# A weight staging copy after every fourteenth attention step instead of every ninth

## The chip, the cores and the metric

The kernel runs on the 8 cores of one Trainium2 chip. Each core takes 1,024 of the 8,192 tokens and runs the same program; nothing is exchanged between cores. The metric is the device time of the slowest core in microseconds (us).

## The reference

A layer in three parts, on x of 2 x 4096 tokens and 4096 features:

```python
x = x + 0.5 * ffn(layernorm(x))     # low-rank experts, rank 8*16 = 128, softmax router over 8
x = x + attn(layernorm(x))          # 32 heads of 128, 8 KV heads, 8192 cached keys
x = x + 0.5 * ffn(layernorm(x))

def attn(h):
    q = rope(h @ Wq)                          # Wq 4096 x 4096
    K, V = kv_cache[block_table]              # 8 KV heads, each serves 4 query heads
    ctx = softmax(q @ K.T / sqrt(128)) @ V
    return ctx @ Wo                           # Wo 4096 x 4096
```

## The kernel before

Activations lie transposed: 32 tiles of 128 features by 512 tokens. A core's 1,024 tokens are two chunks of 512, and the chunks run one after the other (`for c in range(NCH)`). A chunk is: layer norm (`emit_LN`), low-rank part (`emit_FFN`), layer norm, query projection with rotation (`emit_QT`), attention (`emit_ATT`), output projection (`emit_WO`, called WO below), layer norm, low-rank part, store. Instructions are put by hand on one in-order stream for each engine (`PE`, `AC`, `DV`, `GP` for GpSimd, which the profile calls POOL, and `SY` for SyncE, which it calls SP); waits are counts of semaphores.

**Attention.** There are 8 KV heads g, for each 4 query heads, and for each of these 32 groups of two key blocks. A group is two score matmuls (L511), one exponential over both (L518), two matmuls that sum the weights (L539) and two that apply the values (L551), these four in `flush_group`, which runs two groups late. So a chunk has 8 x 4 x 32 = 1,024 calls of `flush_group`, 128 for each g, and `flushctr` counts them. Keys and values of one g fill `KT` and `VT`, in 4 slabs of 16 blocks. There is no second buffer: a slab of g + 1 is loaded by GP (L472, L479) once the fourth query head of g is through with the slab of g, that is at calls 103, 111, 119 and 127 of the 128. For the last g nothing is loaded, so the last slab of a chunk is issued at call 895.

**Staging copies.** Both projections need a weight matrix in bf16. In chunk 0 the query projection reads it from the f32 input, with a cast in the DMA. For the rest (WO of both chunks, the query projection of chunk 1) the kernel makes bf16 copies in DRAM during chunk 0. The queue `pc_queue` holds 64 blocks of wo and then 64 of wq. `precast_pump(1)` takes one block: GP issues a casting load of 512 KB as counted after the cast, wo or wq to the one buffer `PCB` (L458), which waits until PCB is free; SP issues the plain store from PCB to `wob` or `wqb` (L464), which waits for the load; PCB is free when the store has landed. So the copies are one serial chain, load, store, load, and each load sits in GP's stream in front of whatever GP is to do next. None of them waits for the progress of attention. GP's stream is put together in program order, so a pump stands between the slab loads as the call counter places it.

What is left in `pc_queue` after the last call of `flush_group` is issued at once (`while pc_queue: precast_pump(1)`), in GP's stream ahead of the squares of the next layer norm. WO reads `wob` with DMAs of ACT's queue into the two halves of `WB`, and waits for the copies of wo alone (`pco_done.get("o")`). WO adds each result tile to X on DVE (L626).

**Layer norm.** For each of 32 tiles: DVE casts X to XN (L198), GP squares it into the single buffer `SQr` (L202), PE sums both (L209, L217). The square of a tile waits until PE has read the one before.

Of the kernel before, what the change touches and what calls it, by code (L numbers as in the profile page):

```python
# [73 lines left out]
def build_program():  # L74
# [35 lines left out]
    with ctx:  # L110
# [46 lines left out]
        def bw(b):  # L157
            return free.get(("pb", b))

        def tile(buf, i, w=CH):  # L160
            return buf[:, i * w:(i + 1) * w]
# [286 lines left out]
        def precast_pump(n=1):  # L448
            for _ in range(n):
                if not pc_queue:  # L450
                    return
                which, blk = pc_queue.pop(0)
                i, hh = blk // 2, blk % 2
                w_d = wo_d if which == "o" else wq_d
                dst_d = wob_d if which == "o" else wqb_d
                osem = sPCOo if which == "o" else sPCOq
                GP.add(
                    (lambda i=i, hh=hh, w_d=w_d: lambda g: g.dma_start(  # L458
                        PCB[:, :].rearrange("p (j m) -> p j m", j=16),
                        w_d.rearrange("(j p) m -> p j m", p=128)  # L460
                        [:, hh * 16:(hh + 1) * 16, i * 128:(i + 1) * 128]))(),
                    waits=[free.get(("pcb",))], inc=sPCI, inc_amt=16)
                v = SY.add(
                    (lambda blk=blk, dst_d=dst_d: lambda s: s.dma_start(  # L464
                        dst_d[blk], PCB[:, :]))(),
                    waits=[(sPCI, sPCI.val)], inc=osem, inc_amt=16)
                free[("pcb",)] = (osem, v)
                pco_done[which] = (osem, v)

        def emit_kv_slab(c, g, s, ktv, vtv):  # L470
            v = GP.add(
                (lambda g=g, s=s: lambda gp: gp.dma_start(  # L472
                    KT[:, s * SLAB * 128:(s + 1) * SLAB * 128],
                    kt_d[g * 128:(g + 1) * 128,
                         s * SLAB * 128:(s + 1) * SLAB * 128]))(),
                waits=[free.get(("kvslab", s))], inc=sKT[s], inc_amt=16)
            ktv[(g, s)] = (sKT[s], v)
            v = GP.add(
                (lambda g=g, s=s: lambda gp: gp.dma_start(  # L479
                    VT[:, s * SLAB * 128:(s + 1) * SLAB * 128]  # L480
                    .rearrange("p (j d) -> p j d", j=SLAB),
                    vt_d.rearrange("(j p) d -> p j d", p=128)
                    [:, g * NK + s * SLAB:g * NK + (s + 1) * SLAB, :]))(),
                waits=[free.get(("kvslab", s))], inc=sVT[s], inc_amt=16)
            vtv[(g, s)] = (sVT[s], v)
# [5 lines left out]
        flushctr = [0]  # L491

        def emit_ATT(c, po_qt):
# [32 lines left out]
            def flush_group(item):  # L526
                g, qh, grp, gg, ac_e = item
                h = g * 4 + qh
                cb = 2 + (h % 2)
                lb = 4 + (h % 2)  # L530
                slot = (2 * gg) % NPS
                pe_L = pe_ctx = None
                for t in range(2):
                    j = 2 * grp + t
                    wl = [(sAC, ac_e)]
                    if j == 0:
                        wl.append(bw(lb))
                    pe_L = PE.add(
                        (lambda lb=lb, slot=slot, t=t, j=j: lambda tt: tt.matmul(  # L539
                            BNK[lb], ONES[:, :],  # L540
                            PS4[:, (slot + t) * CH:(slot + t + 1) * CH],
                            start=(j == 0), stop=(j == NK - 1)))(),
                        waits=wl, inc=(sPE if j == NK - 1 else None))
                    wc = [vtv[(g, j // SLAB)]]
                    if j == 0:
                        wc.append(bw(cb))
                    need_inc = (t == 1) and (
                        (qh == 3 and (j % SLAB) == SLAB - 1)
                        or grp == NK // 2 - 1)
                    pe_ctx = PE.add(  # L550
                        (lambda g=g, j=j, slot=slot, t=t, cb=cb: lambda tt: tt.matmul(  # L551
                            BNK[cb], VT[:, j * 128:(j + 1) * 128],
                            PS4[:, (slot + t) * CH:(slot + t + 1) * CH],
                            start=(j == 0), stop=(j == NK - 1)))(),
                        waits=wc, inc=(sPE if need_inc else None))
                    if qh == 3 and t == 1 and (j % SLAB) == SLAB - 1:
                        free[("kvslab", j // SLAB)] = (sPE, pe_ctx)
                        if g + 1 < NG:
                            emit_kv_slab(c, g + 1, j // SLAB, ktv, vtv)
                if flushctr[0] % 9 == 0:  # L560
                    precast_pump(1)
                flushctr[0] += 1
                if grp == NK // 2 - 1:
                    ac_lnl = AC.add(
                        (lambda lb=lb: lambda sc: sc.activation(
                            MB[:, :], BNK[lb], AF.Ln))(),
                        waits=[(sPE, pe_L), free.get(("mb",))], inc=sAC)
                    free[("pb", lb)] = (sAC, ac_lnl)
                    ac_rl = AC.add(lambda sc: sc.activation(  # L569
                        RSD[:, :], MB[:, :], AF.Exp, scale=-1.0),  # L570
                        waits=[(sAC, ac_lnl), free.get(("rsd",))], inc=sAC)
                    free[("mb",)] = (sAC, ac_rl)
                    dv_c = DV.add(
                        (lambda h=h, cb=cb: lambda v: v.tensor_tensor(  # L574
                            tile(QC, h), BNK[cb], RSD[:, :], ALU.mult))(),
                        waits=[(sPE, pe_ctx), (sAC, ac_rl)], inc=sDV)
                    free[("pb", cb)] = (sDV, dv_c)
                    free[("rsd",)] = (sDV, dv_c)
                    dv_ctx[h] = dv_c

            for g in range(NG):
                for qh in range(4):
                    for grp in range(NK // 2):
                        gg, ac_e = emit_scores_group(g, qh, grp)
                        pending.append((g, qh, grp, gg, ac_e))
                        if len(pending) > 2:
                            flush_group(pending.pop(0))
                while pending:
                    flush_group(pending.pop(0))
# [186 lines left out]
```

How the kernel before makes its waits and increments, by code:

```python
    def replay(self, eng):  # L63
        for fn, waits, inc, amt in self.ops:
            for s, v in waits:
                eng.wait_ge(s.h, v)
            if fn is None:
                continue
            instr = fn(eng)
            if inc is not None:
                instr.then_inc(inc.h, amt)
```

## Time and profile before

| | us |
|---|---|
| median of 3 runs | 4906.14 (4897.51 to 5272.22) |
| profiled execution, device time | 4920.42 |
| its slowest core, span (core 0) | 4918.9 |
| spans of the 8 cores | 4845.2 to 4918.9 |
| mean granted clock of TensorE, 8 cores | 0.901 to 0.908 |

The engines over that span: PE busy 4061.0 us (83%), ACT 2345.8 us (48%), POOL 776.0 us (16%), DVE 686.7 us (14%). The rows below come from core 0 of this execution unless their caption names another. A "wait" row says how long an engine was idle ahead of an instruction until the named releaser; a timeline row gives start, duration, instruction, and in brackets the idle time ahead of it. A DMA instruction on POOL is its issue; its bytes land later.

### The profile page before, as it was taken

What the parts mean: (1) busy time and instruction counts of PE and PEld (TensorE: products, weight loads), DVE (VectorE), ACT (ScalarE), POOL (GpSimd) and SP (SyncE); (2) the same over time, 40 slices, a digit from 0 to 9 for tenths busy, and PEclk for the clock granted to TensorE, in tenths of its full rate; (3) what the DMA queues carried; (4) which work ended last, traced back from release to release, by engine and by line L of the source; (5) the groups of instructions that cost most, each with busy time, mean ns of one, the idle gap of its engine ahead of it and who ended that gap; (6) DMA issues with size and microseconds to landing.
All of it is one profiled execution on the core that took longest, in us unless ns stands there. A gap on an engine that the chain in (4) does not pass through costs nothing.

```text
span 4918.9 us, 46299 instructions; the slowest of 8 cores (4845.2 to 4918.9 us)
## 1 busy us (share of the span) xinstructions
PE 4061.0 (83%) x16880; PEld 1701.4 (35%) x17224; DVE 686.7 (14%) x937; ACT 2345.8 (48%) x2193; POOL 776.0 (16%) x722
## 2 busy tenths in 40 slices
PE   2556669999999899896773549999999999999985
PEld 0112224444444344342320114444444444444431
DVE  2531120000000000000026553300000000000025
ACT  0000008787788787770000000088888888887000
POOL 4541120111111111100023560000000000000004
PEclk9768789999999999998975559999999999999995
DMA  4148886766776776767614015302220221120432
GB/s 82 17 44 77 77 86 103 105 95 101 112 111 97 111 100 99 106 106 162 159 64 150 13 32 153 120 1 35 35 26 9 35 35 15 20 35 20 140 115 77
DMA packets 616055, 378.54 MB, mean 77 GB/s; under 512 B 549024, under 2 KB 549024, under 8 KB 615840
## 3 DMA queue, kind: packets, MB, share of 16 engines
q0 software_dynamic: 551392, 174.22, 34.3%
q10 hardware_dynamic: 27360, 99.63, 6.0%
q1 hardware_dynamic: 37088, 101.73, 5.4%
q8 instruction: 147, 2.41, 0.2%
q14 instruction: 68, 0.56, 0.0%
HBM read 465.83 MB, written 83.89 MB: 112 GB/s over the span
## 4 chain that ended last, share of the span: by engine, by line
PE 46%; DMA 35%; POOL 9%; issue 5%; ACT 2%; DVE 1%; SPq 1%; another core or an unknown queue 0%; POOLq 0%; ACTq 0%; DVEq 0%
DMA PCB<-wo 12%; PE pc L551 9%; PE pl L539 9%; PE psA L615 7%; PE psA L422 7%; DMA PCB<-wq 6%; PE psA L511 5%; PE psB L511 5%; DMA wob<-PCB 5%; DMA WB<-wq 4%; POOL SQr L202 4%; DMA WB<-wob 4%; DMA wqb<-PCB 3%; POOL XN L260 2%; PE pl L217 2%
## 5 line engine op out<-in xcount | busy, mean ns | idle before, releaser
L518 ACT ACTIVATE PS<-psA,CST 128x1024 bf16<-128x1024 f32 x1024 | 1139.8, 1113 | 1014.2 <-PE psA L511 1007.0
L551 PE MATMUL pc<-PS,VT 128*128 128x512 bf16 x4013 | 1531.2, 382 | 7.9 <-DMA VT<-vt 3.6
L539 PE MATMUL pl<-PS,ONES 128*128 128x512 bf16 x4013 | 1532.8, 382 | 4.6 <-issue 0.2
L518 ACT ACTIVATE PS<-psB,CST 128x1024 bf16<-128x1024 f32 x1024 | 1140.6, 1114 | 198.9 <-PE psB L511 188.6
L422 PE MATMUL psA<-XN,WB 128*128 128x512 bf16 x2008 | 535.8, 426 | 222.3 <-DMA WB<-wq 148.3
L511 PE MATMUL psA<-QC,KT 128*128 128x512 bf16 x2006 | 607.2, 383 | 105.4 <-DMA KT<-kt 73.6
L511 PE MATMUL psB<-QC,KT 128*128 128x512 bf16 x2010 | 608.5, 383 | 7.4 <-DVE UR L376 5.2
L551 PEld LDWEIGHTS pc<-PS,VT 128*128 128x128 bf16 x4096 | 403.1, 98 | 497.5 <-issue 21.2
L539 PEld LDWEIGHTS pl<-PS,ONES 128*128 128x128 bf16 x4096 | 403.4, 98 | 491.9 <-issue 16.4
L615 PE MATMUL psA<-QC,WB 128*128 128x512 bf16 x2006 | 475.4, 394 | 91.6 <-DMA WB<-wob 85.6
L238 ACT ACTIVATE G<-RSD,CST 128x512 f32<-128x512 f32 x6 | 4.3, 721 | 1017.0 <-DVE RSD L232 1017.0
L574 DVE TENSOR_TENSOR QC<-pc,RSD 128x512 bf16<-128x512 f32 x64 | 44.3, 692 | 2763.0 <-ACT RSD L569 2763.0
L422 PEld LDWEIGHTS psA<-XN,WB 128*128 128x128 bf16 x2048 | 213.6, 106 | 541.2 <-issue 364.4
L202 POOL TENSOR_TENSOR SQr<-XN 128x512 bf16<-128x512 bf16 x192 | 210.8, 1098 | 789.0 <-DVE XN L198 626.6
L615 PEld LDWEIGHTS psA<-QC,WB 128*128 128x128 bf16 x2048 | 200.2, 100 | 367.0 <-issue 161.5
L511 PEld LDWEIGHTS psA<-QC,KT 128*128 128x128 bf16 x2048 | 195.5, 98 | 364.1 <-issue 142.6
L511 PEld LDWEIGHTS psB<-QC,KT 128*128 128x128 bf16 x2048 | 202.1, 99 | 252.7 <-issue 15.6
L217 PE MATMUL pl<-SQr,ONES 128*128 128x512 bf16 x188 | 109.4, 582 | 181.9 <-POOL SQr L202 181.9
L472 POOL DMA_DIRECT2D KT<-kt x64 | 36.1, 564 | 1371.8 <-PE pc L551 1371.8
L209 PE MATMUL pl<-XN,ONES 128*128 128x512 bf16 x190 | 119.0, 626 | 90.3 <-DVE XN L198 85.2
L458 POOL DMA_DIRECT2D PCB<-wq x64 | 73.2, 1144 | 751.0 <-DMA wqb<-PCB 713.6
L458 POOL DMA_DIRECT2D PCB<-wo x64 | 73.3, 1146 | 737.4 <-DMA wob<-PCB 719.1
(57 smaller groups left out, 1401.6 us busy)
## 6 DMA issues: line engine op xcount, KB each, us to landing
WB<-wob ACTq DMA_DIRECT2D x128, 512.0 KB, 3.3
WB<-wq POOLq DMA_DIRECT2D x66, 512.0 KB, 7.3
KT<-kt POOLq DMA_DIRECT2D x64, 512.0 KB, 10.4
VT<-vt POOLq DMA_DIRECT2D x64, 512.0 KB, 14.1
PCB<-wo POOLq DMA_DIRECT2D x64, 512.0 KB, 7.8
wob<-PCB SPq DMA_DIRECT2D x64, 512.0 KB, 3.0
PCB<-wq POOLq DMA_DIRECT2D x64, 512.0 KB, 8.3
wqb<-PCB SPq DMA_DIRECT2D x64, 512.0 KB, 3.4
```

The lines of the kernel that those rows point to most:

```text
L202: (lambda i=i: lambda g: g.tensor_tensor(SQr[:, :], tile(XN, i), tile(XN, i), ALU.mult))(),
L209: (lambda i=i: lambda t: t.matmul(BNK[4], ONES[:, :], tile(XN, i), start=(i == 0), stop=(i == DT - 1)))(),
L217: (lambda i=i: lambda t: t.matmul(BNK[5], ONES[:, :], SQr[:, :], start=(i == 0), stop=(i == DT - 1)))(),
L260: (lambda i=i, sl=sl: lambda e: e.tensor_tensor(tile(XN, i), tile(TTr, sl), RSDB[:, :], ALU.mult))(),
L422: (lambda i=i, j=j, b=b: lambda t: t.matmul(BNK[b], WB[:, (0 if j < 16 else 2048) + (j % 16) * 128: (0 if j < 16 else 2048) + (j % 16) * 1 ...
L458: (lambda i=i, hh=hh, w_d=w_d: lambda g: g.dma_start(PCB[:, :].rearrange("p (j m) -> p j m", j=16), w_d.rearrange("(j p) m -> p j m", p=12 ...
L511: (lambda j=j, b=lo + t, h=h: lambda tt: tt.matmul(BNK[b], KT[:, j * 128:(j + 1) * 128], tile(QC, h), start=True, stop=True))(),
L518: (lambda slot=slot, big=big: lambda sc: sc.activation(PS4[:, slot * CH:(slot + 2) * CH], big[:, :], AF.Exp, bias=CST[:, 0:1], scale=ISQ))(),
L539: (lambda lb=lb, slot=slot, t=t, j=j: lambda tt: tt.matmul(BNK[lb], ONES[:, :], PS4[:, (slot + t) * CH:(slot + t + 1) * CH], start=(j == 0 ...
L551: (lambda g=g, j=j, slot=slot, t=t, cb=cb: lambda tt: tt.matmul(BNK[cb], VT[:, j * 128:(j + 1) * 128], PS4[:, (slot + t) * CH:(slot + t + ...
L574: (lambda h=h, cb=cb: lambda v: v.tensor_tensor(tile(QC, h), BNK[cb], RSD[:, :], ALU.mult))(),
L615: (lambda i=i, j=j, b=b: lambda t: t.matmul(BNK[b], WB[:, (0 if j < 16 else 2048) + (j % 16) * 128: (0 if j < 16 else 2048) + (j % 16) * 1 ...
```

## The change

The pump is called after every fourteenth call of `flush_group` instead of every ninth:

```diff
@@ -557,7 +557,7 @@
                         free[("kvslab", j // SLAB)] = (sPE, pe_ctx)
                         if g + 1 < NG:
                             emit_kv_slab(c, g + 1, j // SLAB, ktv, vtv)
-                if flushctr[0] % 9 == 0:
+                if flushctr[0] % 14 == 0:
                     precast_pump(1)
                 flushctr[0] += 1
                 if grp == NK // 2 - 1:
```

The number of copies (128) and their order stay. Counted from the code, for the calls 0 to 1,023 of chunk 0:

| | every 9th | every 14th |
|---|---|---|
| pumps placed in attention | 114 | 74 |
| pumps per g (128 calls) | 14.2 | 9.1 |
| pumps ahead of the last slab load (call 895) | 100 | 64 |
| pumps behind the last slab load | 28 | 64 |
| of these behind the last call | 14 | 54 |

## Rows read from the trace of the kernel before

**Rows 1.** Page, the chain that ended last: shares by line.

```profile
DMA PCB<-wo 12%; PE pc L551 9%; PE pl L539 9%; PE psA L615 7%; PE psA L422 7%; DMA PCB<-wq 6%; PE psA L511 5%; PE psB L511 5%; DMA wob<-PCB 5%; DMA WB<-wq 4%; POOL SQr L202 4%; DMA WB<-wob 4%; DMA wqb<-PCB 3%; POOL XN L260 2%; PE pl L217 2%
```

**Rows 2.** Waits of POOL, whole span: us in total, times, longest.

```profile
POOL KT L472 <- PE pc L551: 1371.8, 28, 377.5
POOL PCB L458 <- DMA wob<-PCB: 728.8, 63, 36.6
POOL PCB L458 <- DMA wqb<-PCB: 713.6, 61, 16.0
```

**Rows 3.** Stages, both attentions, WO of both chunks: us, busy, PEclk, DMA share, GB/s.

```profile
733.00:2195.00 1462.00, 1358.89 (x6022) 604.42 (x6144) 25.60 (x38) 1166.39 (x1088) 174.83 (x167) 0.97 0.71 103
2197.00:2510.00 313.00, 241.84 (x972) 99.77 (x992) 21.23 (x31) 0.00 (x0) 18.29 (x16) 0.91 0.67 159
3181.00:4530.00 1349.00, 1324.45 (x6014) 598.68 (x6138) 24.22 (x36) 1166.04 (x1086) 47.81 (x56) 1.00 0.18 23
4535.00:4780.00 245.00, 228.73 (x1008) 97.86 (x1029) 27.44 (x42) 0.00 (x0) 3.16 (x3) 0.99 0.40 135
```

**Rows 4.** Waits of PE from 720 to 2200 us, the attention of chunk 0.

```profile
PE psA L511 <- DMA KT<-kt: 73.6, 17, 6.7
```

**Rows 5.** Timeline of POOL, copies away from slab loads and beside one.

```profile
957.13 1.14 POOL L458 DMA_DIRECT2D PCB<-wo  x1 [9.56 <-DMA wob<-PCB]
...
1047.84 1.14 POOL L458 DMA_DIRECT2D PCB<-wo  x1 [9.79 <-DMA wob<-PCB]
...
2038.12 1.15 POOL L458 DMA_DIRECT2D PCB<-wq  x1 [12.79 <-DMA wqb<-PCB]
2039.25 0.56 POOL L472 DMA_DIRECT2D KT<-kt  x1
2039.80 1.17 POOL L479 DMA_DIRECT2D VT<-vt  x1
2056.12 1.15 POOL L458 DMA_DIRECT2D PCB<-wq  x1 [15.16 <-DMA wqb<-PCB]
```

**Rows 6.** DMA issues from 957 to 1048 us: count, KB each, us to landing.

```profile
PCB<-wo POOLq DMA_DIRECT2D x9, 512.0 KB, 7.5
wob<-PCB SPq DMA_DIRECT2D x8, 512.0 KB, 3.1
```

**Rows 7.** Timeline of POOL: end of attention, WO of chunk 0, next layer norm.

```profile
2184.52 1.15 POOL L458 DMA_DIRECT2D PCB<-wq  x1 [11.19 <-DMA wqb<-PCB]
...
2403.79 1.15 POOL L458 DMA_DIRECT2D PCB<-wq  x1 [12.96 <-DMA wqb<-PCB]
2518.50 1.08 POOL L202 TENSOR_TENSOR SQr<-XN 128x512 bf16<-128x512 bf16 x1 [113.56 <-DVE XN L198]
```

**Rows 8.** Timeline of POOL, slab loads of keys: slab 0, slab 0, chunk 1's last.

```profile
874.98 0.56 POOL L472 DMA_DIRECT2D KT<-kt  x1
...
1063.14 0.56 POOL L472 DMA_DIRECT2D KT<-kt  x1
...
4363.42 0.55 POOL L472 DMA_DIRECT2D KT<-kt  x1 [7.79 <-PE pc L551]
```

**Rows 9.** Page, issues of keys and values: count, KB each, us to landing.

```profile
KT<-kt POOLq DMA_DIRECT2D x64, 512.0 KB, 10.4
VT<-vt POOLq DMA_DIRECT2D x64, 512.0 KB, 14.1
```

**Rows 10.** Score matmuls of each attention: count, duration ns, first and last start.

```profile
L511 PE MATMUL psA<-QC,KT x1003: 376/379/634, 733.0 to 2188.3; 128*128 128x512 bf16 x168
...
L511 PE MATMUL psA<-QC,KT x162: 376/379/634, 3180.3 to 3398.6; 128*128 128x512 bf16 x162
```

**Rows 11.** Timeline of DVE: WO columns 0, 15, 31 of chunk 0.

```profile
2206.24 0.69 DVE L626 TENSOR_TENSOR X<-psA,X 128x512 f32<-128x512 f32 x1 [11.55 <-PE psA L615]
...
2393.77 0.69 DVE L626 TENSOR_TENSOR X<-psA,X 128x512 f32<-128x512 f32 x1 [9.32 <-PE psA L615]
...
2517.33 0.69 DVE L626 TENSOR_TENSOR X<-psA,X 128x512 f32<-128x512 f32 x1 [7.11 <-remote]
```

**Rows 12.** Timeline of POOL: squares of that layer norm, first with the casts beside, then without.

```profile
2520.37 1.07 POOL L202 TENSOR_TENSOR SQr<-XN 128x512 bf16<-128x512 bf16 x1 [0.78 <-PE pl L217]
...
2535.08 1.30 POOL L202 TENSOR_TENSOR SQr<-XN 128x512 bf16<-128x512 bf16 x1 [0.88 <-PE pl L217]
2537.26 1.04 POOL L202 TENSOR_TENSOR SQr<-XN 128x512 bf16<-128x512 bf16 x1 [0.88 <-PE pl L217]
2539.18 1.04 POOL L202 TENSOR_TENSOR SQr<-XN 128x512 bf16<-128x512 bf16 x1 [0.88 <-PE pl L217]
```

**Rows 13.** Copies of wq on cores 0 and 7: duration ns, first and last issue.

```profile
L458 POOL DMA_DIRECT2D PCB<-wq x64: 1140/1142/1157, 1569.9 to 2403.8; - x64
...
L458 POOL DMA_DIRECT2D PCB<-wq x64: 1140/1140/1154, 1527.8 to 2325.4; - x64
```

## The prediction

> **What bounds the kernel now.** I read the chain that ended last first. Four of its entries are staging copies, PCB<-wo, PCB<-wq, wob<-PCB and wqb<-PCB, 26% of the span together [rows 1]. TensorE is busy 83% of the time, yet the chain goes through loads and stores that no matmul of that stage reads. The waits of POOL say why: ahead of 124 of the 128 copy loads it idled for 1,442 us in all, each time until the store of the copy before had landed [rows 2]. So in chunk 0 GP is a serial chain of copies, and everything else in its stream, the slab loads among it, is as late as that chain.
>
> The stages come next. The two attentions do the same work and take 1,462 and 1,349 us [rows 3]; from the first score matmul to the last that is 2188.3 - 733.0 = 1,455 us in chunk 0. In chunk 1 there are no copies, the clock is 1.00 and PE is busy 98% of the stage: that is the attention as PE alone would have it. In chunk 0 PE idled 73.6 us for keys [rows 4], and the clock is 0.97. The two WO stages take 313 and 245 us [rows 3], the first with copies beside it.
>
> The timeline gives the rate of the copies. Away from slab loads, 8 intervals from 957.13 to 1047.84 are 11.3 us each [rows 5]: 7.5 us until the load lands, 3.1 us for the store, and the issues [rows 6]. With a slab's two loads behind the copy it is 2056.12 - 2038.12 = 18.0 us [rows 5]. Beside WO, 16 intervals from 2184.52 to 2403.79 are 13.7 us each [rows 7].
>
> A check that these explain attention 0: 14.2 pumps for each g are 10.2 at 11.3 us and 4 at 18.0 us, 187 us. Slab 0 of g = 1 and of g = 2 were issued at 874.98 and 1063.14, 188 us apart [rows 8]. PE alone needs 1,349 / 8 = 168.6 us per g [rows 3]. So attention 0 runs at GP's pace, about 18 us per g over PE's.
>
> **The change part by part.** No instruction is added or removed; 40 pumps move from between the attention calls to behind them. As GP waits for nothing in a pump but PCB, only a slab load holds it back to PE's pace; after the last slab load (call 895) GP runs through all that is left. So what counts is the time of the last slab load, and the pumps behind it: 28 before, 64 after.
>
> *Step 1, attention.* With 9.1 pumps per g, GP needs at most 9.1 x 18.0 = 164 us and about 5.1 x 11.3 + 4 x 18.0 = 130 us, under PE's 168.6. GP then waits for PE at the slabs, as it does in chunk 1 [rows 2]. Is a slab still in time? It is released two groups late and is needed about 23 groups later, at 168.6 / 128 = 1.32 us a group some 30 us. Keys land in 10.4 us, values in 14.1 us [rows 9], and at most one copy, up to 18 us but in most cases already running, can stand before it. I take the wait for keys as about zero. The bound on the other side is that nothing is gained.
>
> In chunk 1 the last slab was issued 4363.42 - 3180.3 = 1,183 us after the first score matmul [rows 8, 10]. The new last slab is then at 733.0 + 1,183 = 1,916 us instead of 2,039.25 [rows 5], and attention ends at about 733 + 1,349 = 2,082 instead of 2,190. That is a gain of 108 us for the start of WO, and of 123 us for the start of the tail of copies.
>
> *Step 2, the tail.* The first of the 64 pumps is issued at 1,918; 63 intervals follow.
> - Until WO, at 2,086: one of 17 us with the slab beside it and 13 of 11.6 us (128.4 us for 11 intervals from 2056.12 to 2184.52, the same place before [rows 5, 7]), 168 us for 14.
> - Beside WO. Before, columns 0 to 15 of WO, all with copies beside them, took (2393.77 - 2206.24) / 15 = 12.5 us each [rows 11]. Now all 32 have copies beside them: 400 us, from 2,091 to 2,491. At 13.7 us that holds 29 intervals, to about 2,485.
> - The last 20 are alone. The nearest row is the quiet stretch, 11.3 us: 226 us.
> The last copy load is issued at 2,711 us, and the first square of the layer norm stands right behind it, at 2,712.
>
> *Step 3, what waits for it.* Before, GP had issued its last copy at 2403.79 and sat idle 113.56 us until WO's last tile was cast; the first square was at 2518.50 [rows 7]. The copies were free, with 114 us of cover. Now WO is done at 2,491 and the square waits 221 us more: PE's sums wait for the squares, the means for the sums, and the low-rank part, the store, the reload of X and all of chunk 1 for these. Nothing later has slack to take it up; every stage of chunk 1 is behind this one. The shift is 2,712 - 2518.5 = 193 us. The 32 casts on DVE are then long done. Before, the squares beside them came every 2.2 us and later ones every 1.92 us [rows 12]; 8 squares by 0.26 us give back 2 us. Sum: +191 us.
>
> *The gain of step 1 is inside this sum*, not beside it: it moves WO, which is hidden behind the tail, and it starts the tail earlier. The slowdown of WO, from 320 to 400 us, costs nothing, because the tail covers it with 221 us to spare; without that cover it would cost 80.
>
> The profiled execution took 4920.42 us, so its like would be 5,111. It stood 14 us over the median of 4906.14, so the forecast for the median is 5,097 us.
>
> *Bounds of the interval.* The tail is 63 intervals, and each 1 us on the mean is 63 us. All at 11.3 ends at 2,630 (+110 with the 2 us off); all at 13.7 ends at 2,781 (+261). My mean is (2,711 - 1,918) / 63 = 12.6 us. Cores differ: from the first to the last of the wq copies core 0 took 833.9 us and core 7 took 797.6 [rows 13], so 4% less; core 0 should again be the slowest. The Trainium skill (DMA: Bandwidth & Descriptors, section "Issuing engines are not separate DMA queues") says that transfers of all issuers share 16 engines and interleave. The rows agree: the copies slow from 11.3 to 13.7 us beside WO, and WO's columns stretch as well, though they are issued from ACT and the copies from POOL and SP.
>
> **The rivals.**
>
> *The tail is hidden* (the other side). If the copies are done by the time WO ends, nothing waits for them and only the earlier WO is left: 2,491 + 1 against 2518.5, so -26 us, 4,880, not slower. It decides at (2,491 - 1,918) / 63 = 9.1 us an interval. The shortest interval in the rows, idle time and issue together, is 9.56 + 1.14 = 10.7 us [rows 5], and beside WO it must be slower. What speaks for it is only that the cores' memory traffic is spread differently. 3%. The Trainium skill (same page, section "Anatomy of one DMA — SWDGE (gpsimd) path") puts a DMA at 2.0 us plus its bytes over 436e9 per second. For 512 KB that is an estimated 3.2 us, 6.4 us for load and store, and the tail would take 63 x 6.4 = 403 us and be hidden. The trace agrees for the store (3.1 us) and not for the casting load (7.5 us) [rows 6], so I hold to the rows.
>
> *The copies alone are quick.* Once WO is over, no other transfer of this core runs, and neither do the other cores' slab loads. If the last 20 take 10 us and those beside WO 12.5 (32 fit there), the tail ends at 2,491 + 17 x 10 = 2,661: +141 us, 5,047. 12%.
>
> *Attention gains nothing.* If keys come late for another reason, e.g. bandwidth, the last slab stays at 2,039 and the tail of 64 ends at 2,039 + 63 x 12.6 = 2,833: +314 us, 5,220. Against it speaks that attention 1 has no wait for keys with the same loads, and that the copies between slabs become fewer. Half of it (+60 on my number) is likelier than all. 5%.
>
> *The copies slow down.* WO with copies beside it throughout may hold the copies to 15 us or more: 27 fit beside WO, 22 follow, +23 us, 5,120; inside my range.
>
> **How the numbers follow.** The forecast's own mechanism, with intervals near the rows, has 80% and gives 5,060 to 5,140; the quick tail 12%, no gain in attention 5%, the hidden tail 3%. The range 5,045 to 5,150 takes in the quick tail and the slowed copies. This kernel's measurement can tell about 2% from no change, so slower means over 5,004: that takes a shift of 98 us, a mean interval over 11.1 us. The quiet rate is already 11.3 and a third of the tail is beside WO, so slower 94%, within 2% 5%, faster 1%.
>
> **What would show it.** In the profile after: (1) attention 0 takes about 1,350 us, PE's wait for keys there is near zero, and POOL waits at L472 for PE in chunk 0. (2) The last L472 of chunk 0 is near 1,916 us and 64 copy loads follow. (3) WO of chunk 0 ends near 2,490, with about 12.5 us a column to its end. (4) The first square of the next layer norm is at 2,712, right behind the last copy load, and POOL's idle time ahead of it is about zero instead of 114 us; PE idles there some 220 us. (5) From there on every stage takes as long as before. I am wrong if the last copy is issued before WO ends, or if the last slab is much later than 1,916.

## The result: slower by 4%, and the profile after

| | before | after |
|---|---|---|
| undisturbed runs, us | 4897.5 to 4920.3 | 5102.7 to 5124.3 |
| ratio of the undisturbed runs | | 1.0415, 95% interval 1.0392 to 1.0439 |
| span of the slowest core in the profiled execution, us | 4918.9 (core 0) | 5119.0 (core 0) |
| last slab load of chunk 0 (GP), us | 2039.25 | 1922.92 |
| last copy load (GP), us | 2403.79 | 2714.55 |
| last column of WO, chunk 0 (DVE), us | 2517.33 | 2481.53 |
| first square of the next layer norm, us | 2518.50 | 2715.71 |

The forecast was 5,097 us, 1.039 of the median before. (In some executions of either kernel the cores of a die had a lower clock and the time was hundreds of us longer; they are left out of every ratio here, and with them the median over the 10 runs after is 5213.36 us.) The other seven cores show the same shift: their first squares stand at 2,658 to 2,690 us, before at 2,438 to 2,496.

The waits of POOL after, whole span (us in total, times, longest), answer to [rows 2]:

```profile
POOL KT L472 <- PE pc L551: 1857.6, 53, 378.6
POOL PCB L458 <- DMA wqb<-PCB: 716.5, 63, 16.2
POOL PCB L458 <- DMA wob<-PCB: 528.3, 51, 31.0
```

GP now waits for PE ahead of 53 slab loads instead of 28: in chunk 0, too, it arrives early. The waits of PE from 720 to 2100 us no longer have keys among them; their longest row is the ordinary one for the exponential:

```profile
PE psA L511 <- ACT PS L518: 15.7, 30, 1.6
```

The stages after (us, busy time and count of PE, PE's weight loads, DVE, ACT and POOL, granted clock, DMA share, GB/s): attention of chunk 0, WO, the tail alone, and the start of the layer norm, answering to [rows 3]:

```profile
733.00:2090.00 1357.00, 1330.64 (x6036) 601.03 (x6160) 26.00 (x38) 1163.44 (x1086) 136.87 (x134) 1.00 0.61 85
2090.00:2500.00 410.00, 270.40 (x1008) 108.31 (x1027) 33.55 (x65) 1.23 (x2) 34.63 (x29) 0.85 0.76 157
2500.00:2700.00 200.00, 0.00 (x0) 0.00 (x0) 0.00 (x0) 0.00 (x0) 20.54 (x18) 0.50 0.63 94
2700.00:2820.00 120.00, 46.73 (x92) 9.04 (x93) 38.30 (x36) 1.35 (x2) 72.16 (x66) 0.50 0.13 22
```

The third row is the loss. For 200 us PE, DVE and ACT do nothing at all, and GP is busy 20.5 us issuing copies. The granted clock is at its lower level there (0.50, which is 1.2 GHz; PE stands still), and the mean over the span falls from 0.901 to 0.887. The lower mean is no second cause of the loss: from the first square to the end this core takes 2,403.3 us, before 2,400.4. The timeline of POOL at its end, with the last slab load and the first copy behind it at the head, answering to [rows 7]:

```profile
1922.92 0.55 POOL L472 DMA_DIRECT2D KT<-kt  x1 [7.79 <-PE pc L551]
...
1924.61 1.17 POOL L458 DMA_DIRECT2D PCB<-wq  x1
...
2083.89 1.14 POOL L458 DMA_DIRECT2D PCB<-wq  x1 [10.28 <-DMA wqb<-PCB]
...
2479.95 1.14 POOL L458 DMA_DIRECT2D PCB<-wq  x1 [11.17 <-DMA wqb<-PCB]
...
2714.55 1.15 POOL L458 DMA_DIRECT2D PCB<-wq  x1 [9.92 <-DMA wqb<-PCB]
2715.71 1.05 POOL L202 TENSOR_TENSOR SQr<-XN 128x512 bf16<-128x512 bf16 x1
2717.75 1.04 POOL L202 TENSOR_TENSOR SQr<-XN 128x512 bf16<-128x512 bf16 x1 [0.98 <-PE pl L217]
2719.66 1.04 POOL L202 TENSOR_TENSOR SQr<-XN 128x512 bf16<-128x512 bf16 x1 [0.88 <-PE pl L217]
```

The first square has no bracket: GP did not idle ahead of it at all, where before it had 113.56 us to spare [rows 7]. Its input had long been there. The timeline of DVE shows WO's first and last columns and the casts behind them, done at 2,493 us:

```profile
2106.33 0.69 DVE L626 TENSOR_TENSOR X<-psA,X 128x512 f32<-128x512 f32 x1 [13.37 <-PE psA L615]
...
2481.53 0.69 DVE L626 TENSOR_TENSOR X<-psA,X 128x512 f32<-128x512 f32 x1 [9.03 <-remote]
2482.13 10.81 DVE L198 CAST XN<-X 128x512 bf16<-128x512 f32 x32
```

From there the shift is handed on unchanged. Chunk 1's first score matmul was at 3180.3 us [rows 10]; after it is the first of this row (count, duration in ns, first and last start):

```profile
L511 PE MATMUL psA<-QC,KT x1003: 376/379/631, 3378.6 to 4725.0; 128*128 128x512 bf16 x168
```

That is 198 us later, against 197 us for the first square and 200 us for the span.

### The profile page after: what moved, and what is told of

Same layout as the page of the kernel before. It is cut to its first block, busy times and chain, and to the rows that moved or that the text cites. A ratio compares the mean times of both kernels' runs of the same rounds, so it can differ in the third digit from the quotient of the medians.

```text
span 5119.0 us, 46299 instructions; the slowest of 8 cores (5063.1 to 5119.0 us)
## 1 busy us (share of the span) xinstructions
PE 4044.6 (79%) x16880; PEld 1699.6 (33%) x17224; DVE 679.8 (13%) x937; ACT 2342.9 (46%) x2193; POOL 774.4 (15%) x722
## 4 chain that ended last, share of the span: by engine, by line
PE 60%; DMA 22%; POOL 8%; issue 5%; ACT 2%; DVE 1%; SPq 1%; POOLq 0%; ACTq 0%; another core or an unknown queue 0%; DVEq 0%
PE pc L551 15%; PE pl L539 15%; DMA PCB<-wq 10%; PE psA L511 8%; PE psB L511 8%; PE psA L422 7%; DMA WB<-wq 5%; DMA wqb<-PCB 4%; POOL SQr L202 4%; PE psA L615 4%; POOL XN L260 2%; PE pl L217 2%; POOL TTr L256 2%; ACT PS L518 2%; DMA WB<-wqb 1%
## 5 line engine op out<-in xcount | busy, mean ns | idle before, releaser
L615 PE MATMUL psA<-QC,WB 128*128 128x512 bf16 x2006 | 497.6, 406 | 137.3 <-DMA WB<-wob 131.2
L217 PEld LDWEIGHTS pl<-SQr,ONES 128*128 128x128 bf16 x192 | 20.0, 104 | 561.2 <-issue 561.2
```

Of the source, the lines that this page charges most:

```text
L217: (lambda i=i: lambda t: t.matmul(BNK[5], ONES[:, :], SQr[:, :], start=(i == 0), stop=(i == DT - 1)))(),
L615: (lambda i=i, j=j, b=b: lambda t: t.matmul(BNK[b], WB[:, (0 if j < 16 else 2048) + (j % 16) * 128: (0 if j < 16 else 2048) + (j % 16) * 1 ...
```

## The experiments

Each kernel ran beside the kernel before on one chip, in the same rounds; ratios are to the kernel before. The theory (A): GP's in-order stream is the schedule. In attention the slowest of GP's chain and PE sets the pace; behind the last slab load GP runs the rest of the copies without a break, and the layer norm starts when both that tail and WO are over. The rivals: the slowed WO is what costs (B in the first run), copies cost wherever they are made outside attention (B in the second and third), the count of fourteen hurts as such.

### The copies left over are not made

Behind attention, and in chunk 1's query projection:

```diff
-            while pc_queue:
-                precast_pump(1)
+            pc_queue.clear()
@@
-                                wqb_d[2 * i + hh]))(),
+                                wqb_d[(2 * i + hh) % 10]))(),
```

> Every fourteenth call, and the 54 copies left over behind attention are not made at all; chunk 1's query projection reads the ten copied blocks of wq over and over, so its reads are as many and as large but its output is wrong. Theory A (the tail stands in GP's stream ahead of the squares, and that alone costs the time): WO starts near 2,090 us, takes some 245 to 260 us once the 10 copies placed in the last g are done, the first square is near 2,345 instead of 2,716 us, and the time is about 370 us under the changed kernel, 4,735 to 4,760, ratio to before 0.965 to 0.97. Theory B (the loss is in WO, slowed from 313 to about 400 us by copies beside it): only some 150 us come back, 4,950 or more.

Measured: ratio 0.9647 (0.9533 to 0.9761), span 4747.0 us, 372 us under the changed kernel, where 370 was expected. The timeline of POOL on the slowest core:

```profile
2024.13 1.14 POOL L458 DMA_DIRECT2D PCB<-wq  x1 [9.86 <-DMA wqb<-PCB]
2334.00 1.08 POOL L202 TENSOR_TENSOR SQr<-XN 128x512 bf16<-128x512 bf16 x1 [308.73 <-DVE XN L198]
```

The square is where WO lets it be. B falls: had only WO's stretch been the loss, some 150 us would have come back. But this run takes away position and traffic of the copies at once; the third run parts them.

### Eleven instead of fourteen

```diff
-                if flushctr[0] % 9 == 0:
+                if flushctr[0] % 11 == 0:
```

> A pump after every eleventh call: 82 ahead of the last slab load and 46 behind it. Theory A: GP still waits for PE at the slabs (about 158 us of copies and slabs for each g against 168.6), the last slab is near 1,925 us, 45 intervals of about 12.7 us end near 2,497, just when WO with copies beside it ends (2,490). The first square is at 2,495 to 2,510 and the time 10 to 25 us under before, ratio 0.995 to 0.998. Theory B (time grows with each copy moved from attention into or behind WO): 18 of the 36 moved copies cost half of the loss, about 100 us over before, ratio 1.02.

Measured: ratio 1.003 (1.0009 to 1.0052), span 4942.3 us. A missed by some 30 us (it wanted a time under that of before), and B by more (it wanted 1.02). The timelines of DVE and of POOL say where A missed:

```profile
2450.81 0.69 DVE L626 TENSOR_TENSOR X<-psA,X 128x512 f32<-128x512 f32 x1 [6.60 <-PE psA L615]
...
2527.46 1.15 POOL L458 DMA_DIRECT2D PCB<-wq  x1 [8.62 <-DMA wqb<-PCB]
2528.62 1.05 POOL L202 TENSOR_TENSOR SQr<-XN 128x512 bf16<-128x512 bf16 x1
```

The last slab was at 1,909 us, the first copy behind it at 1,930, and the 45 intervals took 13.3 us each on the mean, not 12.7; the tail ended 30 us after the time expected. WO ended at 2,451 rather than 2,490. So the tail, though expected to be even with WO, outlived it by 77 us. The mechanism stands, and a difference of two long terms was sized too finely.

### The same copies, the last 23 of them inside the layer norms

Fourteen again. 31 copies are issued behind attention; `emit_LN` takes the rest, in the three layer norms ahead of chunk 1's query projection:

```diff
-            while pc_queue:
-                precast_pump(1)
+            if c == 0:
+                precast_pump(31)
@@ emit_LN, behind the square and its matmul; behind a normalisation on GP
+                if spread and i % 6 == 5:
+                    precast_pump(1)
+                    if spread and i in (8, 16, 24):
+                        precast_pump(1)
```

> Every fourteenth call, with only 31 of the leftover copies issued behind attention; the other 23 are placed in GP's stream inside the next three layer norms, one after every sixth square and three among the normalisations, about 11 us apart. The copies and their traffic are those of the changed kernel, all before the query projection of chunk 1. Theory A: the squares start when WO ends, near 2,490 us, 23 issues of 1.15 us in GP's stream cost 27 us and some short waits for the buffer 10 to 30 more; time 4,900 to 4,950, ratio 1.00 to 1.01, against 1.04 of the changed kernel. Theory B (the copies cost time wherever they lie outside attention): it stays at 1.03 to 1.045.

Measured: ratio 0.9977 (0.995 to 1.0003). All 128 copies are made, 64 of them behind the last slab load as in the changed kernel, and its loss is gone. The timeline of POOL on the slowest core:

```profile
2473.81 1.08 POOL L202 TENSOR_TENSOR SQr<-XN 128x512 bf16<-128x512 bf16 x1 [46.34 <-DVE XN L198]
...
2483.83 1.31 POOL L202 TENSOR_TENSOR SQr<-XN 128x512 bf16<-128x512 bf16 x1 [0.88 <-PE pl L217]
2485.09 1.44 POOL L462 DMA_DIRECT2D PCB<-wq  x1
2486.54 1.09 POOL L202 TENSOR_TENSOR SQr<-XN 128x512 bf16<-128x512 bf16 x1
```

A copy between two squares delays them by less than its issue takes: 2483.83 to 2486.54 is 2.7 us, where 2.2 us lie between two squares without it. It waits for nothing, since some 12 us lie between two copies and its buffer is free again. Over the three layer norms the 23 copies cost 13 to 20 us (from the first square to chunk 1's query projection this core takes 400 us, the cores of the kernel before 380 to 387). So it is not the copies' traffic, nor that they are made outside attention. It is that in the changed kernel they stand in GP's stream in one block ahead of work that needs GP.

### A second buffer for the copies

```diff
+                k = pc_n[0] % 2
+                pc_n[0] += 1
+                buf = PCB[:, :] if k == 0 else XN[:, 0:2048]
+                isem, osem = sPCI[k], sPCO[(which, k)]
@@
-                if flushctr[0] % 9 == 0:
+                if flushctr[0] % 8 == 0:
```

Load and store use `buf`, `isem` and `osem`. Whoever waited for the copies of a matrix waits for both semaphores, and the casts of the next layer norm into these four tiles wait for the last store out of them.

> A second buffer for the copies (the first four tiles of XN, which nothing uses from the query projection to the next layer norm), with semaphores of its own, so that a load runs while the copy before is stored; a pump after every eighth call, so all 128 are placed in attention. Theory A (a chain of load and store, 7.5 + 3.1 us, sets the rate): a copy takes about 8 us, 16 copies and 4 slabs of a g fit under PE's 168.6 us, attention 0 takes 1,350 us, no copy is left beside WO, which takes 245 us; 108 + 68 us less than before, about 4,735, ratio 0.965. Theory C (the DMA engines set the rate, busy 71% of attention 0 before): a copy stays at 10 us or more, keys come late, attention 0 stays over 1,420 us and the time over 4,830.

Measured: ratio 0.9659 (0.9585 to 0.9733), span 4749.3 us, the fastest kernel of the study that computes the whole result. The stages on its slowest core, attention of chunk 0 and WO, columns as above:

```profile
733.00:2090.00 1357.00, 1328.78 (x6028) 600.17 (x6152) 24.34 (x36) 1165.18 (x1088) 191.90 (x182) 1.00 0.87 123
2090.00:2335.00 245.00, 224.18 (x997) 96.73 (x1016) 23.89 (x35) 0.00 (x0) 1.08 (x1) 1.00 0.40 133
```

All 128 copies now fit beside an attention at PE's pace. The DMA engines are busy 87% of it, against 71% before [rows 3], and keys are still in time. C falls. The 15 intervals behind the last slab load have a mean of 7.5 us. This run changes the buffer and the count at once; the run with fourteen and the second buffer, below, keeps the changed kernel's count.

### Ten and eight instead of nine

The same line as in the second run, with 10 and with 8.

> A pump after every tenth call: 12.8 for each g, 90 ahead of the last slab load and 38 behind it. Theory A (both sides of the balance decide, GP's pace in attention and the tail behind it): 8.8 copies at 11.2 us and 4 with slabs at 17.5 us are 169 us for each g, just PE's 168.6, so attention 0 takes 1,350 to 1,365 us; the tail of 37 intervals at 13 us ends near 2,410, before WO does (near 2,455); first square near 2,460 us, time 45 to 60 us under before, ratio 0.988 to 0.991, better than nine, eleven or fourteen. Theory B (more copies in attention are always the better): at or over before, ratio 1.00.

> A pump after every eighth call: 16 for each g, 112 ahead of the last slab load and 16 behind it. Theory A: 12 copies at 11.3 us and 4 at 18 us are 208 us for each g, 40 over PE's; the last slab comes near 2,150 us, attention ends near 2,320 us, the 16 copies left are done near then, and WO has the DMA engines nearly to itself, 250 us; first square near 2,575 us, 55 us over before, ratio 1.01 to 1.015. Theory B (thinner pumps are what hurts in the changed kernel, denser ones help): under before, ratio below 1.

Measured: ten 0.993 (0.9896 to 0.9965), eight 1.0135 (1.0083 to 1.0188). With ten the attention is at PE's pace and the tail ends 54 us before the square can start (timeline of POOL, slowest core):

```profile
2420.18 1.15 POOL L458 DMA_DIRECT2D PCB<-wq  x1 [11.66 <-DMA wqb<-PCB]
2475.30 1.08 POOL L202 TENSOR_TENSOR SQr<-XN 128x512 bf16<-128x512 bf16 x1 [53.98 <-DVE XN L198]
```

The ratio is a little short of the 0.988 to 0.991 expected, since WO ended at 2,474 and not at 2,455. With eight the tail is short, and the loss is in attention instead, in the waits of PE from 720 to 2330 us:

```profile
PE psA L511 <- DMA KT<-kt: 180.4, 27, 14.1
```

So the time is lowest in between and rises to both sides: 1.0135, 1, 0.993, 1.003, 1.0415 for 8, 9, 10, 11 and 14. No theory in which more copies beside attention are always better, or always worse, gives this.

### Fourteen with the second buffer

> The changed kernel's count of fourteen with the second buffer and its semaphores: the same 64 copies behind the last slab load, but a load runs while the copy before is stored. Theory A (what hurts is the length of the tail, so it is harmless where a copy is quick): beside attention 7.5 us a copy as with the second buffer before, beside WO 9 to 10 us; 22 copies until WO starts, the other 42 end near 2,480 us, WO ends between 2,430 and 2,490; first square within 10 us of WO's end, time 30 to 80 us under before, ratio 0.985 to 0.995. Theory B (the count of fourteen hurts by itself): over before, ratio 1.02 or more.

Measured: ratio 1.0011 (0.9988 to 1.0034), span 4909.8 us. The count is that of the changed kernel, 64 copies stand behind the last slab load, and the loss is gone: the tail takes 8.3 us a copy instead of 12.5 and ends at 2,435, ahead of WO (timelines of POOL and of DVE, slowest core):

```profile
2435.14 1.15 POOL L465 DMA_DIRECT2D XN<-wq  x1 [2.16 <-DMA wqb<-XN]
2484.73 1.08 POOL L204 TENSOR_TENSOR SQr<-XN 128x512 bf16<-128x512 bf16 x1 [48.45 <-DVE XN L199]
...
2483.56 0.69 DVE L636 TENSOR_TENSOR X<-psA,X 128x512 f32<-128x512 f32 x1 [7.20 <-remote]
```

The count does not hurt by itself, only through the length of the tail. The time missed the expected 0.985 to 0.995: WO's columns took (2483.56 - 2102.59) / 31 = 12.3 us with the copies beside them, so WO ended at the late end of the range given. Attention ended about 100 us earlier than in the kernel before and the first square came 34 us earlier: some two thirds of that gain had gone into a slower WO. Of the 34 us only 9 are left in the span, since this core takes 2,425 us from its first square to the end, and the cores of the kernel before 2,400 to 2,416. That difference stays unexplained.

### The same bytes in long runs

```diff
-                        PCB[:, :].rearrange("p (j m) -> p j m", j=16),
-                        w_d.rearrange("(j p) m -> p j m", p=128)
-                        [:, hh * 16:(hh + 1) * 16, i * 128:(i + 1) * 128]))(),
+                        PCB[:, :],
+                        w_d[i * 128:(i + 1) * 128,
+                            hh * 2048:(hh + 1) * 2048]))(),
```

> The changed kernel, but each copy load reads 128 rows of 2,048 neighbouring f32 instead of 16 runs of 128 f32 in each partition, with the same bytes and the same cast; the copies hold other blocks of the matrices, so the output is wrong. Theory A (short runs make the casting load take 7.5 us): the load lands in 3 to 5 us, a copy takes 7 to 8.5 us alone, the tail of 64 ends near 2,430 us, before WO does, and the time is at or under before, ratio 0.985 to 1.0. Theory D (the cast or the memory makes it 7.5 us): the load stays at 7 us or more and the ratio stays near 1.04.

Measured: ratio 1.0158 (1.0106 to 1.021), between the two. DMA issues of this kernel from 2520 to 2570 us, when the copies are alone (count, KB each, us to landing):

```profile
wqb<-PCB SPq DMA_DIRECT2D x6, 512.0 KB, 2.7
PCB<-wq POOLq DMA_DIRECT2D x6, 512.0 KB, 5.3
```

and those of the changed kernel from 2530 to 2710 us:

```profile
wqb<-PCB SPq DMA_DIRECT2D x16, 512.0 KB, 2.6
PCB<-wq POOLq DMA_DIRECT2D x16, 512.0 KB, 7.6
```

Short runs are 2.3 of the load's 7.6 us, so D, which wanted 7 us or more, falls; a copy alone takes 8.5 us instead of 11.2. The load's remaining 5.3 us, twice the store's, stay unexplained between the cast, the f32 bytes that it reads and GP's issue. No run parted these. The expectation had a copy alone right at its upper end and missed those beside WO, which took 11.7 us. So the tail ended at 2,574 us and not at 2,430, and the first square stood right behind it: 141 us earlier than in the changed kernel, 56 us later than before. The time follows in the main, which is once more the theory of the tail: 62% of the loss is gone by the ratios. In the spans 112 of the 141 us arrive, since this core takes 2,433 us from its first square to the end (six of the eight cores take 2,407 to 2,416); the other 29 us stay unexplained. The size of the effect of run length is smaller than A had it.

## Why the prediction was right, step by step

*Step 1, attention at PE's pace*: right. From the first score matmul (741.2 us) to the last slab load it took 1,181.7 us, against 1,183 read off chunk 1. PE's wait for keys fell from 73.6 us to nothing. That the chain of GP, and not the traffic, held attention back is shown by the two-buffer kernel with a count of eight: more DMA activity beside attention (87% against 61%), and PE busy 1,328.8 us of the same 1,357 us, against 1,330.6.

*Step 2, the tail*: right in sum (ended at 2,714.55 instead of 2,711), and nearly so in each part. The agreement to 4 us owes something to luck. The stretch until WO was forecast 9 us too long and the stretch alone 9 us too short, and these cancel; and attention began 8 us later in this execution than in the one before.

| part of the tail | forecast | measured |
|---|---|---|
| until WO | 14 intervals, 168 us | 14 intervals, 1924.61 to 2083.89: 159 us, 11.4 each |
| beside WO | 29 at 13.7 us | 28, 2083.89 to 2479.95: 396 us, 14.1 each |
| alone | 20 at 11.3 us | 21, 2479.95 to 2714.55: 235 us, 11.2 each |

WO's columns took (2481.53 - 2106.33) / 31 = 12.1 us against 12.5. The row taken from 16 columns with copies beside them held for 32, within 4%.

*Step 3, what waits*: right. The first square stands 1.16 us behind the last copy load, the squares come every 1.9 to 2.0 us from the start on, and the shift of 197 us runs to the end. All five signs named are in the rows above (WO ended 9 us earlier than named). The slowed WO was forecast to cost nothing, as the tail covers it. The third and seventh runs, where the tail is out of the way and WO takes its 370 to 380 us, show what it is worth without that cover: there the first square comes 34 to 45 us before that of the kernel before, though attention ended some 100 us earlier.

The forecast of +191 us compares with 200 in the profiled spans and about 4.15% of 4,911, 204 us, in the runs. The 4 us between 193 and 197 are the tail's, less than the 8 us of the later attention. The 2 us that quicker squares were to give back do not show: from the first square to the end it took 3 us more than before. The rest lies within the spread of single executions (some 22 us in either kernel), and nothing here tells more.

*The rivals.* The hidden tail, with its break-even at 9.1 us a copy, did not happen, but the two-buffer kernel with the count of fourteen made it happen: 8.3 us a copy, and the loss was gone. The copies alone were not quick (11.2 us, not 10), attention gained what was forecast, and beside WO the copies slowed to 14.1 us, not to 15. The estimate of 6.4 us a copy from the Trainium skill (DMA: Bandwidth & Descriptors, section "Anatomy of one DMA — SWDGE (gpsimd) path") is not reached by long runs either (8.5 us). That section gives its fit for transfers issued by GpSimd, and the prediction used it for SP's store as well, where the trace happens to agree (3.1 us). The same page, section "Why small descriptors are slow (HBM only)", lays a penalty on small descriptors; the last experiment agrees in direction, with 7.6 us in short runs against 5.3 in long ones for the same bytes.

*Slips that changed nothing.* "A third of the tail is beside WO" should be nearly half (29 of 63 intervals), which only strengthens "slower". In the rival of the slowed copies, 27 intervals of 15 us and 22 of 11.3 end 29 us later than the forecast's tail, not 23; 5,126 us is inside the range as well.

## What to carry to other kernels

Background work put into an in-order stream has two prices: in front of the loads that it delays, and as a block behind the last instruction that holds it back. Thinning it out moves it from the first to the second. There the wait of GP's next work is zero up to the cover (114 us here) and full after that. But the block is not free under its cover: its transfers slow the stage beside it. The two-buffer kernels differ in the count alone, and with eight, where no copy is left beside WO, the span is 4749.3 us, with fourteen 4909.8. So work out both ends, count by count, before choosing the interval. Shortening the chain itself (a second buffer, 11.2 to 7.5 us a copy, with the count of eight that this allows) was worth 3.4%; the best of the five counts tried with one buffer was worth 0.7%.

## What the runs showed of the hardware

The DMA engines had more room than a share of 71% in attention suggested: with 87% busy, keys and values still came in time. Beside WO the streams slow each other, and how much depends on the run length of the copies as well as on their rate:

| beside WO | a copy, us | a column of WO, us |
|---|---|---|
| one buffer, short runs (changed kernel) | 14.1 | 12.1 |
| two buffers, short runs | 9.2 | 13.2 |
| one buffer, long runs | 11.7 | 9.9 |
| copies over (last four columns, two buffers) | | 7.1 to 7.9 |
| no copies (first run) | | 7.4 |

With two copies in flight a column of WO took 1.1 us longer, and the copies came 4.9 us closer together. With long runs both got shorter. Not all of a longer column is waiting for the transfer, though. In the changed kernel's WO (2092 to 2482 us) PE waited 118.7 us for `wob` and was busy 269.2 us at a mean granted clock of 0.86; without copies (first run, 2090 to 2333 us) it waited 11.9 us and was busy 228.5 us at 0.99. So of the 147 us between the two stages 107 are waiting and 41 are the same matmuls taking longer (431 ns each on the mean, against 381) at the lower mean clock. That a transfer of another queue is slowed by the run length of its neighbour was not expected; what it shares with it (the engines' time or something on the way to memory) was not tried.
